# An expert kernel's low weight parts: requests moved to the first group of the expert before, and a wait by table

## What is computed

```python
logits = x @ w_router.T
probs = jax.nn.softmax(logits, axis=-1)
expert_weight, expert_idx = jax.lax.top_k(probs, TOP_K)      # TOP_K = 2, E = 8
...
inter = jnp.square(jax.nn.relu(jnp.einsum('ecd,efd->ecf', binned, w1_stack)))
outb = jnp.einsum('ecf,edf->ecd', inter, w2_stack)
...
return shared_out + moe_out
```

## Time and profile before

| | us |
|---|---|
| median of 3 runs | 1275.64 (1274.3 to 1278.38) |
| the profiled execution, its time | 1274.7 |
| its span | 1273.0 |
| TensorE busy | 1242.2 (98%) |
| VectorE busy | 756.4 (59%) |
| ScalarE busy | 376.9 (30%) |
| POOL busy | 206.5 (16%) |
| the 16 DMA engines, SyncE's queue | 71.0% of their span |

### The profile page before, as it was taken

The page is one execution under the profiler, slowest core; times in us unless marked ns, Lnnn a source line. Parts: engine busy times, 40 slices in busy tenths (PEclk is TensorE's granted clock), DMA queues, the critical chain, the costliest instruction groups (busy, mean ns, idle before and its releaser), DMA issues.

```text
span 1273.0 us, 22853 instructions
## 1 busy us (share of the span) xinstructions
PE 1242.2 (98%) x7814; PEld 860.7 (68%) x7815; DVE 756.4 (59%) x1421; ACT 376.9 (30%) x613; POOL 206.5 (16%) x176
## 2 busy tenths in 40 slices
PE   6999999999999999999999999999999999999997
PEld 3344444444444444467888888899999888877886
DVE  4456555655454444478988877857546355555554
ACT  2322211212121111244554554442323233333322
POOL 0000000000000000004222223610531012222222
PEclk9999999999999999999999999999999999999999
DMA  9999999999999999833787778840643777776775
GB/s 356 417 422 418 417 418 422 422 423 422 417 404 412 391 391 395 317 139 132 268 290 258 266 278 309 280 105 4 230 166 131 208 220 187 187 153 153 184 155 94
DMA packets 105434, 358.39 MB, mean 282 GB/s; under 512 B 19873, under 2 KB 40353, under 8 KB 90785
## 3 DMA queue, kind: packets, MB, share of 16 engines
q1 hardware_dynamic: 96880, 337.97, 71.0%
q0 software_dynamic: 8496, 19.73, 7.7%
HBM read 352.80 MB, written 67.78 MB: 330 GB/s over the span
## 4 chain that ended last, share of the span: by engine, by line
PE 81%; DMA 9%; DVE 4%; issue 2%; SPq 1%; ACT 1%; POOL 0%; ACTq 0%; DVEq 0%; POOLq 0%
PE ps L2000 14%; PE ps L1888 13%; PE ps L2072 11%; PE ps L2062 9%; DMA parts_low<-split 5%; PE ps L2362 5%; PE ps L2354 5%; PE ps L2357 5%; PE ps L1963 4%; PE ps L1846 3%; PE ps L1978 2%; DMA arena<-ctx_n 2%; DMA high<-parts_low 1%; PE ps L1938 1%; PE ps L1945 1%
## 5 line engine op out<-in xcount | busy, mean ns | idle before, releaser
L2072 PE MATMUL ps<-split 128*128 128x256 f32 x1536 | 194.2, 285 | 3.1 <-DVE split L1335 2.7
L2072 PEld LDWEIGHTS ps<-split 128*128 128x128 f32 x1536 | 187.1, 191 | 8.0 <-issue 6.4
L2000 PE MATMUL ps<-arena 128*64 128x512 f32 (+1 forms) x832 | 192.3, 594 | 0.0
L1888 PE MATMUL ps<-arena 128*64 128x512 f32 (+1 forms) x1024 | 178.6, 505 | 2.3 <-DMA arena<-ctx_t 1.6
L1888 PEld LDWEIGHTS ps<-arena 128*64 128x64 f32 x1024 | 65.7, 138 | 122.7 <-issue 119.7
L2000 PEld LDWEIGHTS ps<-arena 128*64 128x64 f32 (+1 forms) x832 | 58.3, 137 | 112.4 <-issue 111.7
L1231 DVE SCALAR_TENSOR_TENSOR arena<-arena,hbar 128x512 f32<-128x512 f32 x128 | 90.5, 750 | 67.8 <-PE ps L1963 66.1
L767 ACT ACTIVATE arena<-ps 128x512 f32<-128x512 f32 (+1 forms) x93 | 52.3, 581 | 240.1 <-PE ps L1963 180.2
L757 POOL DMA_INDIRECT out<-arena,token_i x39 | 60.5, 1552 | 246.5 <-DVE arena L1802 135.3
L651 POOL TENSOR_TENSOR arena<-arena,row_b 128x512 f32 (+1 forms) x16 | 20.3, 1271 | 474.3 <-DVE arena L1105 446.4
L2062 PE MATMUL ps<-split 128*128 128x512 f32 x384 | 96.9, 401 | 0.0
(11 more groups left out here) (249 smaller groups left out, 1947.0 us busy)
## 6 DMA issues: line engine op xcount, KB each, us to landing
arena<-ctx_t SPq DMA_DIRECT2D x122, 800.5 KB, 15.3
high<-parts_low SPq DMA_DIRECT2D x78, 1024.0 KB
arena<-ctx_n SPq DMA_DIRECT2D x96, 768.0 KB, 12.1
arena<-ctx_n SPq DMA_DIRECT2D x32, 1024.0 KB, 13.0
parts_high<-split SPq DMA_DIRECT2D x16, 1024.0 KB, 8.7
parts_low<-split SPq DMA_DIRECT2D x16, 1024.0 KB, 10.6
moe_in<-zero SPq DMA_DIRECT2D x3, 3328.0 KB, 19.0
stage_raw<-w1t SPq DMA_DIRECT2D x8, 1024.0 KB, 6.6
```

Source lines behind the costliest of these rows:

```text
L1888: last = mm(bank(n)[S * h:S * (h + 1), 0:w], qT[:, k, S * h:S * (h + 1)], ctxT[h][:, k, at_j:at_j + w], start=(k == 0), stop=(k == KD - 1))
L2000: last = mm(bank(7)[S * h:S * (h + 1), :], ET[0:w, c, S * h:S * (h + 1)], ctxN[h][0:w, c, :], start=(c == 0), stop=(c == JC - 1))
L2072: last = mm(dst[:, 2 * P * m:2 * P * (m + 1)], w[a][:, k, c], tokens[b][:, k, :], start=(k + i == 0), stop=(k == KD - 1 and i == 2))
```

## The change

Three tables are made or replaced. need_i is read by TensorE in place of eg_i: beside the expert and the place it holds the value of low1_back (or low2_back) to wait for, 16 times (one more than the count of loads up to the one that brings this expert's weights). next_i is read by SyncE: the expert that follows the one of group g, with its place, and a bit (16) that is set only at the first group of an expert that has a successor. VectorE makes both in run_starts, with 19 further operations. SyncE's load for index g + 1 now brings the *next expert's* weights, at the first group of the present one; all others are skipped. Each call reads its table itself, behind the wait that stands before it, and waits as before until the load before it has landed.

```diff
-            def load_low(g, parts, places, back):
-                odd, e = group[g] >= E, group[g] & (E - 1)
-                if g > 0:
-                    sp.wait_ge(back, 16 * g)
+            def load_low(value, parts, places, back, at, cond):
+                odd, e = (value & (2 * E - 1)) >= E, value & (E - 1)
+                if at > 0:
+                    sp.wait_ge(back, 16 * at)
                 sp.dma_start(all_high[:, bass.ds(places[0] + odd * (places[1] - places[0]), KD * D)].bitcast(F32),
-                             parts[bass.ds(e * P, P), :], cond=group[g] != group[g - 1] if g > 0 else None
-                             ).then_inc(back, 16)
+                             parts[bass.ds(e * P, P), :], cond=cond).then_inc(back, 16)
+            def first_low(parts, places, back):
+                value = sp.value_load(eg_i[0:1, 0:1], min_val=0, max_val=2 * E - 1)
+                load_low(value, parts, places, back, 0, None)
+            def next_low(g, parts, places, back):
+                value = sp.value_load(next_i[0:1, g:g + 1], min_val=0, max_val=4 * E - 1)
+                load_low(value, parts, places, back, g + 1, value >= 2 * E)
...
-            read_group(1)
             sp.wait_ge(shlo_used, 1)
-            load_low2(0)
+            first_low(*second)
             sp.wait_ge(shared_done, TA)
-            load_low1(1)
+            next_low(0, *first)
             sp.wait_ge(x3_ready, T)
             store_rows(slice(TR, T))
             for g in range(GT):
                 if g + 2 < GT:
-                    read_group(g + 2)
                     sp.wait_ge(in_done, g + 1)
-                    load_low1(g + 2)
+                    next_low(g + 1, *first)
                 if g + 3 < GT:
                     sp.wait_ge(xgT_ready, g + 2)
                     load_slots(g + 3)
                 if g + 1 < GT:
                     if g > 0:
                         sp.wait_ge(y_done, g)
-                    load_low2(g + 1)
+                    next_low(g, *second)
+            sp.wait_ge(low1_back, 16 * GT)
+            sp.wait_ge(low2_back, 16 * GT)
```

In run_starts (VectorE), behind its first three operations:

```diff
+                step(v.tensor_tensor(gcmp, run.unsqueeze(2).to_broadcast([P, GT, E]),
+                                     ends.unsqueeze(1).to_broadcast([P, GT, E]), ALU.is_gt))
+                step(v.tensor_tensor(gcmp, gcmp, ends.unsqueeze(1).to_broadcast([P, GT, E]), ALU.mult))
+                step(v.tensor_reduce(rank, gcmp, AX, ALU.max))
+                step(v.tensor_scalar(landed, run, 0.0, None, ALU.is_gt))
+                step(v.tensor_tensor(rank, rank, landed, ALU.add))
+                step(v.scalar_tensor_tensor(eg_f, rank, 2.0 * E, eg_f, ALU.mult, ALU.add))
+                v.tensor_scalar(need_i, eg_f, 2.0 * E, None, ALU.add).then_inc(token_ready, 1)
+                step(v.tensor_tensor(gcmp, ends.unsqueeze(1).to_broadcast([P, GT, E]),
+                                     iota_g.unsqueeze(2).to_broadcast([P, GT, E]), ALU.is_le))
+                step(v.scalar_tensor_tensor(gcmp, gcmp, 4.0 * GT, ends.unsqueeze(1).to_broadcast([P, GT, E]),
+                                            ALU.mult, ALU.add))
+                step(v.tensor_reduce(rank, gcmp, AX, ALU.min))
+                step(v.tensor_tensor(gcmp, ends.unsqueeze(1).to_broadcast([P, GT, E]),
+                                     rank.unsqueeze(2).to_broadcast([P, GT, E]), ALU.is_le))
+                step(v.tensor_reduce(eg_f, gcmp, AX, ALU.add))
+                step(v.tensor_scalar(eg_f, eg_f, float(E - 1), None, ALU.min))
+                step(v.scalar_tensor_tensor(eg_f, turn, -float(E), eg_f, ALU.mult, ALU.add))
+                step(v.tensor_tensor(landed, run, iota_g, ALU.is_equal))
+                step(v.tensor_scalar(rank, rank, float(GT), None, ALU.is_lt))
+                step(v.tensor_tensor(landed, landed, rank, ALU.mult))
+                step(v.scalar_tensor_tensor(eg_f, landed, 2.0 * E, eg_f, ALU.mult, ALU.add))
+                v.tensor_scalar(next_i, eg_f, float(E), None, ALU.add).then_inc(token_ready, 1)
```

The waits for token_ready on SyncE and POOL, which counted these tables, count two more. On TensorE:

```diff
-                    e, odd = expert(g)
+                    e, odd, need = expert(g)
...
-                         lambda: pe.wait_ge(low1_back, 16 * g + 16))).then_inc(in_done, 1)
+                         lambda: pe.wait_ge(low1_back, need))).then_inc(in_done, 1)
...
-                         lambda: pe.wait_ge(low2_back, 16 * g)),
+                         lambda: pe.wait_ge(low2_back, need_last)),
...
-                group = pe.value_load(eg_i[0:1, bass.ds(g, 1)], min_val=0, max_val=2 * E - 1)
-                return group & (E - 1), group >= E
+                value = pe.value_load(need_i[0:1, bass.ds(g, 1)], min_val=2 * E, max_val=2 * E * (GT + 3) - 1)
+                return value & (E - 1), (value & (2 * E - 1)) >= E, value & -2 * E
+            pe.wait_ge(token_ready, 2 + NY)
             experts(0, last=False)
```

More of the change, by code:

```diff
@@ L109, in perceiver_layer @@
         eg_i = sb("eg_i", [P, GT], I32)
+        next_i = lg[:, :, :].rearrange("p t e -> p (t e)")[:, 0:GT].bitcast(I32)
+        need_i = causal[:, 0:GT].bitcast(I32)
         token_i = sb("token_i", [P, GT], I32)
@@ L545, in _ @@
             store_rows(slice(TH // 2, TH))
[L547 to L551, removed]
-            def load_low(g, parts, places, back):
-                odd, e = group[g] >= E, group[g] & (E - 1)
-                if g > 0:
-                    sp.wait_ge(back, 16 * g)
-                sp.dma_start(all_high[:, bass.ds(places[0] + odd * (places[1] - places[0]), KD * D)].bitcast(F32),
-                             parts[bass.ds(e * P, P), :], cond=group[g] != group[g - 1] if g > 0 else None
-                             ).then_inc(back, 16)
[L562 to L568, removed]
+            def load_low(value, parts, places, back, at, cond):
+                odd, e = (value & (2 * E - 1)) >= E, value & (E - 1)
+                if at > 0:
+                    sp.wait_ge(back, 16 * at)
+                sp.dma_start(all_high[:, bass.ds(places[0] + odd * (places[1] - places[0]), KD * D)].bitcast(F32),
+                             parts[bass.ds(e * P, P), :], cond=cond).then_inc(back, 16)
[5 more added lines that the diff above has]
+                load_low(value, parts, places, back, g + 1, value >= 2 * E)
+            first = parts_low[0], LOW1, low1_back
+            second = parts_low[1], LOW2, low2_back
             sp.wait_ge(x3_out, 32)
             load_w2(ARENA + KD * D, 7, 8)
-            sp.wait_ge(token_ready, NY)
+            sp.wait_ge(token_ready, 2 + NY)
             load_w2(3 * KD * D, 3, 4)
@@ L579, in _ @@
                 sp.wait_ge(scat[i], 32 * (T // NH))
-            load_low1(0)
+            first_low(*first)
             def load_slots(g):
@@ L747, in _ @@
                         ).then_inc(scat[i], 16)
-            pool.wait_ge(token_ready, 1 + NY)
+            pool.wait_ge(token_ready, 3 + NY)
             pool.wait_ge(x3_out, 16 * 4)
@@ L2382, in experts @@
                         (lambda: pe.wait_ge(xhi_ready, g + 1), lambda: pe.wait_ge(xlo_ready, g + 1),
-                         lambda: pe.wait_ge(low1_back, 16 * g + 16))).then_inc(in_done, 1)
+                         lambda: pe.wait_ge(low1_back, need))).then_inc(in_done, 1)
                 if last:
-                    e_last, odd_last = expert(g - 1)
+                    e_last, odd_last, need_last = expert(g - 1)
                     if second:
```

## The result

| | before | after |
|---|---|---|
| median of the runs taken side by side (us) | 1274.3 (19 runs) | 1280.21 (19 runs) |
| ratio, 95% interval | 1 | 1.0039 [1.0029, 1.005] |
| profiled execution (us) | 1274.7 | 1281.4 |
| its span (us), mean granted clock | 1273.0, 0.998 | 1279.7, 0.995 |

The ratio means 5.0 us more, between 3.7 and 6.4. The forecast was 1.7 us more. So the change makes the kernel slower. The middle of the interval, 0.39%, lies over the 0.3% set as the bound of "no change"; its lower end, 0.29%, lies just under it.

A forecast was written before the change was run, and what follows sets the result against it. TensorE, busy 98% of the span, bounds the kernel, so only its idle time can be won. Terms -2.0 + 1.4 + 2.3 = +1.7 us give 1277.3 us on the median 1275.64; range 1273.6 to 1281.0.

The forecast's parts named there:

- The two low-part waits go: -2.0: Experts' stage: TensorE's two waits for low parts vanish because weights are requested three or four groups earlier; 2.0 us gained.
- VectorE's tables: run_starts: 19 added operations take 6.3 us, delay pair 6's low parts, and TensorE stands still 1.4 us near 975 us.
- the second stop: Start of experts' stage: group 3's slots go out 5.7 us late behind the request's landing; TensorE waits 2.3 us.
- +2.3 (start): TensorE's wait at the start of the experts' stage, group 3's slots being late; 2.3 us, bounds 0.7 to 4.2.
- TensorE's queue: 0: Wait by table on TensorE: same operations ahead of a group's first matmul, so 0 us; other bound 3.7 us.
- Rival (c): TensorE's queue exposed: 0.1 us in each of 37 groups, 3.7 more than forecast, +5.4, 1281.0 us; chance 0.05.
- second slots: 0: Group 4's slots, behind the second-layer low part: nothing more lost at 7.2 us after its request; at 8.4, 1.2 us.
- (b): Slow landings: SyncE's wait ahead of group 3's slots, flight 8.4 us, group 4's slots late too; +4.8, 1280.4 us; chance 0.13.
- (a): Quick landings: request lands in 4.9 us, TensorE waits 0.7 instead of 2.3; sum +0.1, 1275.7 us; chance 0.15.
- (e): All collisions are covered, only the two low-part waits go; -2.0, 1273.6 us; chance 0.10.
- (d): Wait before the second layer's low parts stays, another thing holding the queue there; +3.7, 1279.3 us; chance 0.04.
- slower by over 0.3%: Outcome class for the whole kernel, more than 0.3% (3.8 us) slower; chance 0.20.

The follow-up runs named there:

- the tables alone: Kernel before plus the 19 table operations in run_starts and two token_ready counts, nothing reading the tables; 1.0019 [1.0007, 1.0032] to the kernel before.
- tables apart: Kernel after with the landed-count tables moved behind the squares and low parts that pairs 5 and 6 wait for; 1.0037 [1.0024, 1.005] to the kernel before.
- slots ahead: Kernel with tables apart, no request ahead of the loop, slots before both next-expert requests in every group; 1.0027 [1.0008, 1.0046] to the kernel before.
- the filler: Kernel after, groups 2 to 4 written out on TensorE, eight unread matmuls queued behind group 2; 1.0046 [1.0029, 1.0064] to the kernel before.
- groups 2 to 4 written out: Kernel after with these groups written out on TensorE instead of looped, no added matmuls; one run, 1277.08 us against a median of 1273.49.

## Why the prediction was right and wrong

**Right.** *The two low-part waits go: -2.0.* They went, worth 1.93 here, and no kernel with the early requests has such a wait. That they are worth 2.0 holds for the execution on which the forecast rests; the same kernel run again had one wait, 0.7 us. *VectorE's tables.* 6.3 us forecast, 6.4 measured; a stop of 1.4 forecast, 1.40 measured; +1.70 in all to the first transposes. The run with the tables alone and the one with them apart show it from both sides. The 0.15 us for a restart had no row behind it: from the end of the low parts (977.04 + 1.28) to TensorE's start at 978.56 it is 0.24. *The place and the size of the second stop.* With 3.51 subtracted from the times after: the request at 1035.4 as forecast, its flight 6.7 us for 6.5, the slots at 1042.9 for 1042.5, VectorE's turn at 1046.8 for 1046.65, TensorE late by 2.26 for 2.3. The Trainium skill's fit for one DMA on GpSimd's path ("DMA: Bandwidth & Descriptors", section on the anatomy of one DMA), which the prediction weighed, gives an estimate of 4.4 us. The trace does not agree: the flight took 6.70.

**Wrong: the term "+2.3 (start)".** It was priced as idle time alone. It cost 2.26 + 2.28 = 4.5 us. The second 2.28 reads off the four rows from 1051.66: from the transposes to the first matmul 1.16 us instead of 0.35 (+0.8), then 1.86 and 1.55 for two lines that take 1.01 and 0.92 (+1.5). How much of the first belongs to the clock, a stop at full clock tells: behind the one of 1.56 us in the kernel with slots ahead, where the groups stand in the same loop, it is 1.06 (1054.83 to 1055.89), and the group takes 0.71 more than 5.93. So 0.7 us is a late start, which a stop costs at full clock too, and 1.6 is the half clock. The pair with and without the filler agrees on the clock, 1.5 (7.93 less 5.93 and the late start of 0.5); there both first distances are 0.86, at full and at half clock, so in groups written out the late start is 0.2 to 0.3 smaller. The trace puts the idle time in it down to issue, to no other engine. This one term is 2.2 of the 3.2 us between the forecast and the tail.

**TensorE's queue: 0.** Rival (c), 0.1 in each of 37 groups, is excluded: the groups take 5.93 as before, but for three, 0.3 us in all, in which the first matmul comes 0.46, 0.45 and 0.57 behind the transposes instead of 0.35. It isn't shown that the wait by table costs this: the kernel before, run again, has such groups (0.44 at 1046.89, 0.47 at 1196.38) with no wait ahead of them, and the kernel with groups 2 to 4 written out, which reads the same tables, has none of the three. What else is left of the gap of 3.2 us between 4.9 and 1.7 is small: 0.3 in the restart at 978, 0.3 at the end, 0.1 in the low-part waits.

**Covered by luck: "second slots: 0".** I wrote that nothing more is lost unless the flight takes 8.4 us. TensorE indeed waited for nothing at the next set, but because it had run slowly until then. With the clock kept up it waits 0.33 us for VectorE there, and groups 3 and 4 are each some 0.5 us longer than their work (6.91 less the late start of 0.5, and 6.47, against 5.93).

**The rivals.** The time fell on that of (b), +4.8, but not by its mechanism: it wanted a flight of 8.4 us, and it was 6.7. (a) and (e) fall with the stops, (d) with the missing waits. That a stop could lower the clock stood in none of them, and so the case "slower by over 0.3%" had too little with 0.20: the forecast's own stop of 2.3 us was a candidate for it. That 1280.2 lies inside the stated range is luck as well: its upper part stands there for (b) and (c), and neither happened.

## What to carry to other kernels

On an in-order queue that waits for landings, a request moved earlier drags its wait ahead of everything behind it; list what stands behind that wait and when each is needed, for the first pass of the loop as well. Price a stop of TensorE in front of dense work at its idle time plus a late start (0.5 to 0.7 us here) and, where the clock falls, a slow stretch (1.6 here), together as much again, and look at the granted clock behind each stop that is already in the trace. Nineteen small operations for a table were 6.4 us of VectorE: they go where nothing behind them is needed within that time, or they cost the difference.

## What was not expected of the hardware

- **The clock after a stop.** It stayed at 1.00 over the stop of 1.40 us at 977 (the row below), and fell to 0.50 behind those of 2.02 to 2.14 us in three kernels (after, tables apart, groups written out). The stops of 1.56 us in the slots-ahead kernel and of 1.2 to 1.5 in the one with the tables alone were followed by lines at full speed (1.18 to 1.20 us). No run puts stops of several lengths at one place, so what decides between the two cases isn't shown. The Trainium skill ("TensorE: Matmul & The Clock Gate", section "The HAM clock gate") says that the clock has two levels, 1.2 and 2.4 GHz, the lower one being that of an idle TensorE. The trace agrees on the levels, with 0.50 and 1.00 and averages of both in between, and on the fall for the stops of 2.02 to 2.14 us.

```profile
977.00:979.00 2.00, 0.60 (x4) 0.44 (x4) 2.00 (x5) 0.63 (x1) 0.00 (x0) 1.00 0.87 303
```

- **A set of slots depends on what was asked for ahead of it.** Group 3's set took 3.9 us from issue to VectorE's turn in the kernel after, the next 1 MB request only going out at 1049.92; group 4's, behind one 1 MB request, 5.5 (1052.09 to 1057.56).
- **Two executions differed by 1.8 us ahead of the changed code**, and two executions of the kernel before had 1.3 and 0.7 us of waits for low parts. Comparing spans would have given 6.7 us; the tail gave 4.9 and the timing 5.0.
